# A two-pass mixture of experts behind graph attention: the down weights read in place, tile kinds mixed, twelve slots

## What is computed

```python
x = x + gnn(layernorm(x), adj, a0, a1, a2, a3)      # attention over the nodes of a graph
h = layernorm(x)
probs = softmax(h @ gate_w + gate_b)                # 16 experts
top_probs, top_idx = top_k(probs, 2)                # two experts for each token, weights normalized
expert_out[e] = (silu(h @ w1[e]) * (h @ w2[e])) @ w3[e]     # 128 -> 256 -> 128
x = x + sum over the two chosen experts of weight * expert_out
```

## Time and profile before

| | |
|---|---|
| three timed runs | 822.02, 824.17, 825.97 us; median 824.17 |
| the profiled execution | 820.67 us, of which the span from first to last instruction is 818.7 |
| TensorE, matmuls | 710.3 us busy, 87% of the span |
| VectorE / ACT / GpSimd | 66% / 53% / 63% |
| granted TensorE clock, mean | 0.966 of full |
| DMA | 154.07 MB, 188 GB/s over the span |
| 160 weight copies within the chip | 384.0 KB each |

### The profile page before, as it was taken

One profiled execution on the slowest core, in us unless ns is written; L12 is line 12 of the kernel. 1 busy time (PEld: TensorE's weight loads), 2 busy tenths in 40 slices (PEclk: granted clock), 3 DMA queues, 4 the chain that ended last, 5 costly groups with the idle time before them and its releaser, 6 DMA issues.

```text
span 818.7 us, 17860 instructions
## 1 busy us (share of the span) xinstructions
PE 710.3 (87%) x4420; PEld 572.1 (70%) x4420; DVE 543.1 (66%) x2118; ACT 437.5 (53%) x1075; POOL 514.9 (63%) x664
## 2 busy tenths in 40 slices
PE   3788888888888887697999998977899999999872
PEld 1355555555555555586899998967799999999772
DVE  3779999999999999765666665543444444444231
ACT  4689999999999997232333332322233333333220
POOL 3124777777777777677767675654466666766443
PEclk9889999999999999589999999999999999999997
DMA  7233433332222210267999985888888888858880
GB/s 187 58 91 99 123 118 119 119 114 91 80 83 83 83 40 28 81 209 227 318 306 311 328 279 130 285 287 296 279 265 267 294 276 270 268 155 298 279 300 3
DMA packets 127449, 154.07 MB, mean 188 GB/s; under 512 B 16362, under 2 KB 98545, under 8 KB 127378
## 3 DMA queue, kind: packets, MB, share of 16 engines
q1 hardware_dynamic: 107008, 115.63, 44.5%
q0 software_dynamic: 15616, 34.38, 12.1%
q10 hardware_dynamic: 4754, 3.25, 1.3%
HBM read 52.28 MB, written 41.19 MB: 114 GB/s over the span
## 4 chain that ended last, share of the span: by engine, by line
POOL 28%; issue 27%; PE 20%; SPq 15%; DMA 4%; ACT 3%; DVE 1%; POOLq 1%; DVEq 0%; ACTq 0%
POOL first_list L559 14%; PE psS L1101 9%; SPq L419 5%; PE bank L1124 5%; POOL second_list L571 5%; SPq L415 5%; PE psS L993 4%; POOL norm L542 3%; SPq L401 3%; POOL out_dram L583 2%; ACT late L656 2%; DMA second_list<-xin 2%; PE bank L1113 1%; POOL stage L527 1%; POOL negmean L536 1%
## 5 line engine op out<-in xcount | busy, mean ns | idle before, releaser
L1101 PE MATMUL psS<-xT,late 128*128 128x256 f32 (+1 forms) x1280 | 249.8, 343 | 4.4 <-DMA late<-wts 2.3
L1101 PEld LDWEIGHTS psS<-xT,late 128*128 128x128 f32 x1280 | 202.7, 195 | 21.5 <-issue 4.5
L666 ACT ACTIVATE silu<-psS 128x512 f32<-128x512 f32 x144 | 86.0, 597 | 206.4 <-PE psS L1101 206.4
L583 POOL DMA_INDIRECT out_dram<-xin x144 | 141.6, 983 | 80.4 <-issue 53.5
L571 POOL DMA_INDIRECT second_list<-xin x144 | 141.9, 985 | 79.1 <-issue 52.0
L958 DVE TENSOR_TENSOR hid<-silu,psS 128x512 f32<-128x512 f32 x144 | 98.9, 687 | 134.5 <-PE psS L1101 127.9
L559 POOL DMA_INDIRECT first_list<-stage,slot x128 | 127.3, 994 | 50.3 <-issue 35.8
L993 PE MATMUL psS<-late,hT 128*128 128x512 f32 x256 | 126.6, 640 | 21.9 <-ACT late L656 20.8
L1124 PE MATMUL bank<-late,hid 128*128 128x128 f32 x1024 | 135.8, 276 | 0.1
L964 DVE SCALAR_TENSOR_TENSOR xin<-bank,xin 128x128 f32<-128x128 f32 x288 | 87.8, 346 | 70.3 <-PE bank L1124 64.9
L1124 PEld LDWEIGHTS bank<-late,hid 128*128 128x128 f32 x1024 | 124.6, 192 | 0.4 <-issue 0.4
(11 more groups left out here) (152 smaller groups left out, 913.4 us busy)
## 6 DMA issues: line engine op xcount, KB each, us to landing
late<-wts SPq DMA_DIRECT2D x160, 384.0 KB, 3.8
xin<-second_list SPq DMA_DIRECT2D x48, 262.0 KB
X<-in_x_dram SPq DMA_DIRECT2D x32, 256.0 KB, 2.9
late<-in_adj_dram SPq DMA_DIRECT2D x32, 256.0 KB, 3.4
xin<-first_list SPq DMA_DIRECT2D x48, 134.0 KB
xin<-second_list SPq DMA_DIRECT2D x48, 131.0 KB
wts<-in_L_ffn_w_dram SPq DMA_DIRECT2D x48, 128.0 KB
xin<-first_list SPq DMA_DIRECT2D x48, 67.0 KB
```

Source lines behind the costliest of these rows:

```text
L583: pool.indirect_dma_start(out_rows[:, :], bass.IndirectOffsetOnAxis(ap=xin[:, u, k, DEST:DEST + 1].bitcast(i32), axis=0), xin[:, u, k, 0:D ...
L666: nc.scalar.activation(silu[:, w, :], psG[w], ACT.Silu).then_inc(s_silu[u % TURNS], 1)
L1101: last = mm(out[:, c * W2 + rows.start:c * W2 + rows.stop], at[:, half * H + c * P:half * H + (c + 1) * P], xT[:, w, rows], start=True, st ...
```

## The change

**The third weight in place.** `we` keeps only the gate and up weights (512 numbers a partition, UP). The down matmuls take w3 from `wts`, at an address that TensorE computes: its sequencer reads the tile's word from the table (`pe.value_load`) between the gate and up matmuls and the transposes, cuts out the expert, and adds the offsets. Lone tiles keep constant addresses.

**Twelve slots.** S goes from 8 to 12. A copy takes two thirds of the room, so `late`, which holds them, keeps its size; `xin` grows. A pass has 6 turns of 12 tiles.

The diff, cut:

```diff
@@ -40,17 +40,30 @@
...
     UP = 2 * H
-    S = 8
-    WHOLE = (TOKENS - E * (W2 - 1)) // W2 // S
-    MIXED = (TOKENS // W2 - WHOLE * S) // S
-    LONE = E // 2 // S
-    TURNS_EACH = WHOLE + LONE + MIXED
-    TILES = TURNS_EACH * S
-    BITS = 11
+    S = 12
+    SURE = (TOKENS - E * (W2 - 1)) // W2
+    PAIRS = TOKENS // W2 - SURE
+    TILES = SURE + E // 2 + PAIRS
+    TURNS_EACH = TILES // S
+    BITS = 18
...
+    LAST = 5
+
+    def spread(a, b):
+
+        n, k = len(a) + len(b), len(a)
+        return [a[(i + 1) * k // n - 1] if (i + 1) * k // n > i * k // n else b[i - i * k // n] for i in range(n)]
+
+    wholes = [("whole", i) for i in range(SURE)]
+    lones = [("lone", i) for i in range(E // 2)]
+    mixed = [("mixed", i) for i in range(PAIRS)]
+    first = EARLY_TURNS * S
+    TILE = wholes[:first] + spread(mixed[:-LAST], spread(lones, wholes[first:])) + mixed[-LAST:]
+    COPIES = [sum({"whole": 1, "lone": 0, "mixed": 2}[TILE[i][0]] for i in range(j % S, j + 1, S))
+              for j in range(TILES)]
...
@@ -400,87 +408,87 @@
...
             def rows_of(word):
-                row = ((word & (MARK - 1)) << (P.bit_length() - 1)) + ((word >> BITS) & 1)
-                return nc.s_assert_within(row, 0, ROWS - W2, skip_runtime_bounds_check_because="places lie in their area")
+                return nc.s_assert_within(word & (MARK - 1), 0, ROWS - W2,
+                                          skip_runtime_bounds_check_because="places lie in their area")
...
             def copy_weights(word, u, a):
                 e = (word >> BITS) & (E - 1)
-                sp.dma_start(we[:, u, a, :], wts[:, ds(e * EW, EW)]).then_inc(s_we[u], 16)
+                sp.dma_start(we[:, u, a, :], wts[:, ds(e * EW, UP)]).then_inc(s_we[u], 16)
...
-            def load_mixed(r, n, u):
+            def load_tile(r, j):
+                kind, i = TILE[j]
+                u = j % S
+                wait(sp, s_z[u], (r * TURNS_EACH + j // S) * 32)
+                if kind == "whole":
+                    load_whole(r, whole_word(r, i), u)
                 for a in range(2):
-                    word = unit_word(r, (n - r * TURNS_EACH - LONE) * (2 * S) + (2 * u + a))
-                    load_rows(r, word, u, a)
-                    copy_weights(word, u, a)
-
-            def load_turns(first, end, load):
-                with sp.Fori(first, end) as n:
+                    if kind == "lone":
+                        load_rows(r, lone_word(r, 2 * i + a), u, a)
+                    if kind == "mixed":
+                        word = unit_word(r, 2 * SURE + 2 * i + a)
+                        load_rows(r, word, u, a)
+                        copy_weights(word, u, a)
+
+            def load_whole_turns(r, word_of):
+                with sp.Fori(r * TURNS_EACH + 1, r * TURNS_EACH + EARLY_TURNS) as n:
                     for u in range(S):
                         sp.wait_ge(s_z[u], n * 32)
                         sp.sem_inc(s_turn, 1)
-                        load(n, u)
...
+                        load_whole(r, word_of(r, (n - r * TURNS_EACH) * S + u), u)
...
-            load_turns(EARLY_TURNS, WHOLE, lambda n, u: load_whole(0, n, u, tile_word))
+            sp.wait_ge(s_lone, 1)
+            sp.wait_ge(s_padded[0], (E + 1) * 16)
             sp.wait_ge(s_real, 1)
-            real = [sp.value_load(real_i[0:1, u:u + 1], min_val=(WHOLE + LONE) * 32, max_val=TURNS_EACH * 32)
-                    for u in range(S)]
-
-            sp.wait_ge(s_padded[0], (E + 1) * 16)
-            sp.wait_ge(s_lone, 1)
-            load_lone_turns(0)
-            load_turns(WHOLE + LONE, TURNS_EACH, lambda n, u: load_mixed(0, n, u))
-
-            for u in range(S):
-                sp.wait_ge(s_z[u], real[u])
+            for j in range(EARLY_TURNS * S, TILES - S):
+                load_tile(0, j)
+            real = [sp.value_load(real_i[0:1, u:u + 1], min_val=(TURNS_EACH - 1) * 32, max_val=TURNS_EACH * 32)
+                    for u in range(S - LAST, S)]
+            for j in range(TILES - S, TILES):
+                load_tile(0, j)
+
+            for u in range(S - LAST):
+                sp.wait_ge(s_z[u], TURNS_EACH * 32)
+            for u in range(LAST):
+                sp.wait_ge(s_z[S - LAST + u], real[u])
                 sp.sem_inc(s_turn, 1)
-            for u in range(S):
-                sp.wait_ge(s_z[u], TURNS_EACH * 32)
-                load_whole(1, TURNS_EACH, u, tile_word)
-            load_turns(TURNS_EACH + 1, TURNS_EACH + WHOLE, lambda n, u: load_whole(1, n, u, tile_word))
+            for j in range(S):
+                load_tile(1, j)
+            load_whole_turns(1, whole_word)
             sp.wait_ge(s_padded[1], (E + 1) * 16)
-            load_lone_turns(1)
-            load_turns(TURNS_EACH + WHOLE + LONE, 2 * TURNS_EACH, lambda n, u: load_mixed(1, n, u))
+            for j in range(EARLY_TURNS * S, TILES):
+                load_tile(1, j)
...
@@ -688,11 +693,12 @@
...
-                if j == 2 * S - 1:
-                    act.wait_ge(s_pad, 2)
-                    act.wait_ge(s_padrow, 1)
-
-            tiles(act, tile, 1, 0, ((2 + E // S, pad_first), (2 + 2 * E // S, pad_second)), 2, turn_table)
+                if 4 <= j < 4 + E:
+                    pad(0, first_list, ROW, j - 4)
+                if 4 + E <= j < 4 + 2 * E:
+                    pad(1, second_list, ROW2, j - 4 - E)
...
@@ -956,6 +965,13 @@
...
+                if on(2) and r == 0:
+                    k = (u + 2) % S
+                    wait_in(dve, n, u, 2)
+                    for t in range(2):
+                        last = v.tensor_scalar(xin[:, k, t, ROW:ROW2], xin[:, k, t, 0:D], xin[:, k, t, RSTD:RSTD + 1],
+                                               xin[:, k, t, SHIFT:SHIFT + 1], ALU.mult, ALU.add)
+                    last.then_inc(s_xn[k % TURNS], 1)
                 if on(-1):
...
@@ -1065,36 +1074,46 @@
...
-            def down_whole(r, j):
-                return [we[:, j % S, 0, UP:EW]] * 2
-
-            def down_mixed(r, j):
-                return [we[:, j % S, a, UP:EW] for a in range(2)]
...
+            def expert(word):
+                return (word >> BITS) & (E - 1)
+
+            def experts_early(r, j):
+                return [expert(pe.value_load(etable_i[0:1, ds(2 * j, 1)]))] * 2
...
+            def experts_of(r, j):
+                kind, i = TILE[j]
+                if kind == "lone":
+                    return [2 * i, 2 * i + 1]
+                if kind == "mixed":
+                    return [expert(pe.value_load(table_i[0:1, ds(2 * SURE + 2 * i + a, 1), r])) for a in range(2)]
+                return (experts_whole if r or j >= EARLY_TURNS * S else experts_early)(r, i)
...
+            def weights_of(r, j):
+                kind, i = TILE[j]
+                u, halves = j % S, (slice(0, P), slice(P, W2))
+                if kind == "whole":
+                    wait(pe, s_we[u], (r * COPIES[TILES - S + u] + COPIES[j]) * 16)
+                    return [(we[:, u, 0, :], slice(0, W2))]
+                if kind == "mixed":
+                    wait(pe, s_we[u], (r * COPIES[TILES - S + u] + COPIES[j]) * 16)
+                    return [(we[:, u, a, :], halves[a]) for a in range(2)]
+                return [(wts[:, e * EW:e * EW + UP], halves[a]) for a, e in enumerate((2 * i, 2 * i + 1))]
...
@@ -1102,9 +1121,11 @@
...
+                if experts:
+                    e = experts()
...
@@ -1113,37 +1134,38 @@
...
                     for t in range(2):
                         for c in range(HC):
                             at = c * W2 + t * P
                             last = mm(psY[1 - w][:, t * D:(t + 1) * D], hid[:, 1 - w, at:at + P],
-                                      at_down[t][:, c * D:(c + 1) * D],
+                                      wts[:, ds(e[t] * EW + (UP + c * D), D)],
                                       start=(c == 0), stop=(c == HC - 1))
                     last.then_inc(s_Y[k % TURNS], 1)
 
+            def tile_at(r, j):
+                tile(r, r * TURNS_EACH + j // S, j % S,
+                     (lambda: weights_of(r, j)) if 0 <= j < TILES else None,
+                     (lambda: experts_of(r, j - 1)) if j > 0 else None, j + 1 < TILES)
+
...
+                experts_first = experts_whole if r else experts_early
+                tile_at(r, -1)
...
-                with pe.Fori(n0 + 1, n0 + WHOLE) as n:
+                with pe.Fori(r * TURNS_EACH + 1, r * TURNS_EACH + EARLY_TURNS) as n:
                     for u in range(S):
-                        tile(r, n, u, in_whole, down_whole)
...
+                        tile(r, n, u, lambda: weights_whole(r, n, u),
+                             lambda: experts_first(r, (n - r * TURNS_EACH) * S + u - 1))
+                if r == 0:
+                    pe.wait_ge(s_table, 16)
+                for j in range(EARLY_TURNS * S, TILES + 1):
+                    tile_at(r, j)
...
```

134 lines of the change are left out of this document (49 added, 85 removed).

## The result

| | before | changed |
|---|---|---|
| median (lowest to highest) | 823.1 us (820.49 to 825.97, 4 runs) | **783.72 us** (780.43 to 784.77, 4 runs) |
| profiled execution | 820.67 us, span 818.7 | 784.77 us, span 783.0 |
| DMA | 154.07 MB | 133.30 MB |
| granted TensorE clock, mean | 0.966 | 0.966 |

The ratio of changed to before is 0.9514, 95% interval 0.9468 to 0.956: some 39 us or 4.9% faster.

A forecast was written before the change was run, and what follows sets the result against it. TensorE was taken to bound the kernel except for stalls, the mixed ones from SP's issue queue. 5.8 + 3.0 + 12.1 + 14.2 + 0.8 - 1.0 = 34.9 us off 820.7 gives 785.8, plus 3.5: 789 us, range 783 to 806.

The forecast's parts named there:

- What bounds the kernel: Expert part: TensorE bounds except in gaps; SP's issue queue, 4.0 us per mixed tile against 2.90, more than bandwidth makes mixed stalls.
- Start of pass 1, 5.8 us: Tiles 7 to 16 of pass 1: 5.8 us of stalls would go, as twelve slots need a returned slot 11.4 us later.
- Rival (e): Start of pass 1: GpSimd, still scattering the first list, is late, so slots don't help; 5.8 us stay, 795; chance 0.06.
- 3.0 + 12.1 + 14.2: Stalls in us at pass 1 tiles 47 to 48, 59 to 67, and pass 2 tiles 59 to 71; all would go.
- The lead that I put at 19.9 us: Row loads issued ahead of their tile's matmuls: 8.5 us with eight slots, 19.9 with twelve; 12 us can be lost unseen.
- SP's prices: SP's issue cost: mixed half tile falls from 2.00 to 1.75 us, its weight copy from 0.49 to 0.45.
- The turn, 0.8 us: Between the passes: most of the 19.8 us chain from tile 67 is fixed; 0.8 us saved, bounds nothing and 1.8.
- TensorE's register load, 1.0 us in all: TensorE's sequencer, 160 loads for the third weight: about 1.3 us a tile, mostly hidden behind a wait; 1 us lost in all.
- (b): TensorE's sequencer becomes the bound: register loads or register-addressed matmuls hold up the next transposes; 832 us, slower; chance 0.09.
- VectorE's order, nothing: Normed rows ahead of the last weighted sum on VectorE: two instructions change places, rows aren't late, so no time change.
- The sum: Whole kernel: 34.9 us off the profiled 820.7 gives 785.8; with 3.5 us for timed median above profiled, 789.
- rival (d): The turn gains all 1.8 us and some of the tail after the last tile goes too: 784 us; chance 0.04.

The follow-up runs named there:

- e1: Changed kernel with eight slots instead of twelve and the old order of tile kinds (whole, lone, mixed): 804.61 us, ratio 0.9805 to the kernel before.
- e4: Changed kernel with eight slots, new order, and the third weight copied with the others (384 KB a copy, no TensorE register load): 798.33 us, ratio 0.9721.
- e3: Changed kernel with eight slots instead of twelve, new order of tile kinds kept: 794.9 us, ratio 0.9678 to the kernel before.
- e2: Changed kernel with the old order of tile kinds alone, twelve slots kept: 784.37 us, ratio 0.9553 to the kernel before.
- e10: Changed kernel with words and weight copies of pass 2's first two tiles ahead of the waits for pass 1's last slots: 784.93 us; unaltered beside it 784.35.
- e12: Changed kernel with seven used register loads instead of one on TensorE in each of 96 whole tiles: 970.29 us, ratio 1.1761 to the kernel before.
- e11: Changed kernel with VectorE's old order, weighted sum before normed rows: 786.87 us, ratio 0.9541; the unaltered changed kernel beside it 784.35 us.
- e8: Changed kernel with four more semaphores for GpSimd's scatters: 926.66 us, one run on a slower chip where the kernel before took 937.11 us.

## Why the prediction was right, and where it was off

- *What bounds the kernel.* Right: TensorE but for gaps, and the gaps in the mixed stage are SP's late issues. In e1, with a third of the bytes gone from each copy, 11.4 of 29.3 us of mixed stalls stay (5.2 + 6.2 of 15.1 + 14.2), and what went in pass 2 (8.0 us) is what SP's half loads became cheaper by (7.6). Bandwidth has a smaller part, with eight slots alone: e4 against e3.
- *Start of pass 1, 5.8 us.* Gone, 0.1 left. e1 and e3, with eight slots, keep 6.6 and 7.7, so it is the slots that cure it. Rival (e) had the cause right and the effect wrong: GpSimd is what is late. It scatters the first list almost without a pause until 366.9 us, and the scatters of pass 1 queue behind:

```profile
365.94 0.96 POOL L567 DMA_INDIRECT first_list<-stage,slot  x1 [0.31 <-issue]
367.20 1.00 POOL L579 DMA_INDIRECT second_list<-xin  x1 [0.30 <-issue]
```

  The second scatter of tile 0 is issued 19.4 us after the tile's start, in the kernel before as in the changed one, where a steady tile of the kernel before has 8.7. Scatters that queue follow each other at 1.29 us, so a tile's two take 2.58 of its 2.84, and GpSimd catches up by a quarter of a microsecond a tile. Four more slots give 11.4 us, and cover the delay.
- *3.0 + 12.1 + 14.2.* All gone, by more edits than it took: beside the cheaper copies and steps, twelve slots do it without mixing (e2), and mixing does it without twelve slots (e3). The lead that I put at 19.9 us is 20.0 at tile 47 (rows issued 465.46, matmuls 485.50) and 15.9 at tile 71 (538.75 to 554.66); I had 6.0 us of loss, it is 4.1.
- *SP's prices.* A mixed half at 1.75 us: row loads at 538.75 and 540.45, so 1.70, and e1's average in pass 2 is 1.79. The copy's issue at 0.45: it stayed at 0.49 with fewer bytes. The other steps were thus cheaper than thought.

```profile
538.75 0.34 SPq L429 DMA_DIRECT2D xin<-first_list  x1
539.40 0.49 SPq L423 DMA_DIRECT2D late<-wts  x1
540.45 0.34 SPq L429 DMA_DIRECT2D xin<-first_list  x1
```

- *The turn, 0.8 us.* Mis-sized: 3.1. "Most of this chain is fixed" was the wrong step; both ends of it shrank. From tile 67's start to the first load it was 14.05 us and is 12.36. TensorE has no part in that: tile 67's down matmuls start 4.9 us after its gate and up matmuls in both kernels, here before (563.56) and changed (543.06):

```profile
568.46 1.06 PE L1124 MATMUL bank<-late,hid 128*128 128x128 f32 x8
```

```profile
547.97 1.06 PE L1144 MATMUL bank<-wts,hid 128*128 x8
```

  Its last scatter is issued 8.8 and 8.9 us after the start. What shrank is the time that this scatter takes to land: 4.18 us from its issue before, 2.50 in the changed kernel. In the kernel before SP is still issuing loads and 384 KB copies of the last mixed tiles then; in the changed one the last copy goes out 10.9 us ahead of the scatter. The DMA engines in the two stretches (the last three numbers are clock, DMA share and GB/s):

```profile
573.00:576.50 3.50, 2.32 (x21) 2.35 (x22) 1.81 (x5) 0.41 (x2) 0.32 (x1) 1.00 0.87 321
```

```profile
551.90:554.50 2.60, 2.60 (x26) 2.60 (x25) 1.41 (x4) 0.98 (x2) 2.01 (x2) 1.00 0.28 103
```

  Smaller copies may be enough for this part: in e1 and e3, where SP is late too, the scatter lands in 2.7 us, and in e4, with 384 KB, in 3.1. e10 bears it out from the other side.

  From the first load to the matmuls it was 5.79 us and is 4.38, within the bound I gave. The load lands 2.9 us after its issue before and 3.1 in the changed kernel, so that isn't it. But before, when the rows had landed at 580.46, TensorE was still at the padding tiles 70 and 71, whose own rows had come late, and took up the transposes 2.0 us later; in the changed kernel it is 0.3 us.

```profile
580.38 2.22 PE L1124 MATMUL bank<-late,hid 128*128 128x128 f32 x16
582.44 0.38 PE L1113 MATMUL bank<-ident,xin 128*128 128x128 f32 x2
```

- *TensorE's register load, 1.0 us in all.* Right: the steady tiles of pass 2 lose 0.6 us together. A load takes it 0.29 to 0.99 us, where the nearest rows had 0.25 to 0.93:

```profile
L1084 PEldq TENSOR_LOAD <-table_i x60: 287/307/985, 456.6 to 743.1; - x60
L1091 PEldq TENSOR_LOAD <-table_i x64: 296/304/682, 462.5 to 765.8; - x64
```

The cadence stayed at 2.84 and 2.90, so a matmul whose address comes from a register isn't slower here. (b) was not far off: e12 shows that a whole tile has 1.1 to 1.3 us to spare beyond the one load, and that behind these further loads count in full; e11 shows that some of the address steps come to light when VectorE's order is the old one. No run shows how deep TensorE's queue is. The Trainium skill ("Runtime: NRT & Kernel Launch", section "Instruction fetch mechanics") puts a register load at about 200 ns of the sequencer; the trace doesn't agree: none of TensorE's 160 took less than 287 ns and their mean is 402. The estimate by that page, 32 us if each were exposed, did not come true, since they were covered.
- *VectorE's order, nothing.* Off by 2.5 us: it is a gain (e11). I had looked only at whether rows come in time, not at what TensorE's sequencer has to do behind its wait for them. Within the 35.7 us it stands in stretches that I had already credited to the slots: with the sum first, 2.4 us of stalls stay between tiles 7 and 47. So with the third weight in place the slots don't take all of the 5.8 in VectorE's old order.
- *The tail.* Not foreseen: from the last tile's matmuls to the end 19.48 us instead of 18.09, of which GpSimd's DRAIN is 1.3. It comes with the twelve slots (7264 ns in every trace with eight, 8571 in every one with twelve but e8); what sets its length is open.
- *The sum.* 34.9 us off the span predicted, 35.7 measured. 5.7 + 3.0 + 12.1 + 14.1 gone and 3.1 at the turn, less 0.6 in pass 2's steady tiles, 0.3 at the start of the expert part and 1.4 in the tail, is 35.7. So the total came out within 1 us because the turn's 2.3 us too little and the 1.7 us not foreseen (start and tail) nearly cancel; that is luck. The profiled execution came at 784.77 for 785.8. The remaining distance to 789 is the 3.5 us that I added because three runs of the kernel before had their median above its profiled one; those of the changed kernel have it 1 us below theirs. The result, 784 us, is the time rival (d) gave, but not by its way: the turn gained more than (d) allowed and the tail lost.

## What to carry to other kernels

Count the cost of each transfer on the queue that issues it, register steps and waits included, and compare it with the consumer's time per tile, stage by stage: a stage whose issue costs 4.0 us against 2.9 of work stalls even with bandwidth to spare. A deeper ring and an evener mix of expensive and cheap tiles are two cures for the same deficit; try the cheaper one alone first. Register loads can stand in a matmul queue for nothing as long as their sum stays below what the sequencer waits per tile, and that wait can be read from the trace ahead of the edit; by e11's trace the address steps had better stand ahead of a wait than behind it, which no kernel here tried. And a chain that ends in a DMA isn't fixed: what else is in flight while it lands is part of its length.

## What the runs showed of the hardware

- The issue of a 128-partition copy takes SP 0.49 us whether a piece is 2 or 3 KB; row loads of 128 pieces of 536 bytes take 0.34.
- The last scatter that counts in pass 1 (128 rows) landed 2.5 to 2.7 us after its issue with the DMA engines busy for 26 to 28%, 3.25 at 66% (e10), and 4.18 at 87% (the kernel before).
- Two scatters of a tile take GpSimd 2.58 us, one every 1.29.
- Integer steps on TensorE's sequencer follow each other at 0.095 us though each is recorded with 0.036.
- GpSimd's closing DRAIN took 5.6, 7.3 and 8.6 us in kernels that differ in their number of semaphores, and not in step with it.
- Of the three chips of the experiments two gave the kernel before 823 and 825 us and one 937. In the traces of kernels like the changed one, nearly all of the difference lies in the expert part, which took 555 to 559 us there instead of 413 to 417.
